# Two attention and expert layers on one core: loads, stores and output halves moved across phase ends, and fewer semaphore clears

## The reference

```python
x = x + tanh(g_xattn[l]) * attention_l(layernorm(x), ctx_1024, ctx_1024, Wq, bq, Wk, bk, Wv, bv, Wo, bo)
x = x + tanh(g_ffn[l])   * experts_l(layernorm(x), ...)
```

## Time and profile before

| what | before |
|---|---|
| median of 3 runs | 800.38 us (799.07 to 803.17) |
| profiled execution | 800.45 us |
| its span, first to last instruction | 798.7 us |
| busy: TensorE, its weight loads | 739.7 us (93%), 622.6 us (78%) |
| busy: VectorE, ScalarE, GpSimd | 586.2, 461.2, 372.5 us (73%, 58%, 47%) |
| mean granted TensorE clock | 0.969 of full |
| phases in the span, us | attention 1 to 211, route and experts 1 to 487, attention 2 489 to 683, route 2 to 698, experts 2 to 797 |

### The profile page before, as it was taken

One profiled execution on the slowest core, in us unless ns is written; L12 is line 12 of the kernel. 1 busy time (PEld: TensorE's weight loads), 2 busy tenths in 40 slices (PEclk: granted clock), 3 DMA queues, 4 the chain that ended last, 5 costly groups with the idle time before them and its releaser, 6 DMA issues. The chain is left out here.

```text
span 798.7 us, 17138 instructions
## 1 busy us (share of the span) xinstructions
PE 739.7 (93%) x6750; PEld 622.6 (78%) x6750; DVE 586.2 (73%) x1219; ACT 461.2 (58%) x701; POOL 372.5 (47%) x371
## 2 busy tenths in 40 slices
PE   6999999999899999999999983999999999779995
PEld 5666767666899999999999983656666567779994
DVE  5777777682469898898898862677777767759981
ACT  3476666756267776676676642467666754245640
POOL 5454555123044777676666534545545211033633
PEclk9999999999999999999999995999989999979998
DMA  7110000001059988888888625200000000579732
GB/s 221 31 45 26 29 29 27 29 29 55 27 194 366 271 262 269 267 271 268 254 279 272 183 47 156 72 29 28 16 2 16 15 29 15 175 248 318 202 80 27
DMA packets 47680, 103.44 MB, mean 129 GB/s; under 512 B 9936, under 2 KB 38224, under 8 KB 39920
## 3 DMA queue, kind: packets, MB, share of 16 engines
q0 software_dynamic: 16800, 65.46, 27.5%
q1 hardware_dynamic: 30800, 36.87, 13.9%
HBM read 84.22 MB, written 17.83 MB: 128 GB/s over the span
## 5 line engine op out<-in xcount | busy, mean ns | idle before, releaser
L928 DVE TENSOR_REDUCE mx_a<-ps_max_a 128x2 f32<-128x512 f32 x256 | 164.3, 685 | 43.8 <-PE ps_max_a L1238 42.8
L732 ACT ACTIVATE prob_a<-ps_st_a 128x2048 f32<-128x2048 f32 x64 | 120.1, 1877 | 40.4 <-PE ps_st_a L1257 40.1
L88 PE MATMUL ps_h_e<-xe_t_e,w_e 128*128 128x256 f32 x368 | 106.3, 289 | 6.3 <-DVE xe_t_e L2358 6.3
L90 PE MATMUL ps_h_e<-xe_t_e,w_e 128*128 128x256 f32 x368 | 103.4, 281 | 0.0
L89 PE MATMUL ps_h_e<-xe_t_e,w_e 128*128 128x256 f32 x368 | 103.4, 281 | 0.0
L1238 PE MATMUL ps_max_a<-k_r_a,q_r_a 32*128 32x512 f32 x256 | 86.4, 524 | 4.5 <-DVE mx_a L928 1.4
L90 PE MATMUL ps_y_e<-w_e,h_early 128*128 128x256 f32 x312 | 86.7, 278 | 0.0
L2134 POOL DMA_INDIRECT xe_e<-normalised_weighted,token_of x53 | 61.7, 1164 | 43.6 <-DMA normalised_weighted<-comb_first 18.3
L1257 PE MATMUL ps_st_a<-q_s_a,k_s_a 32*128 32x256 f32 x1024 | 79.8, 404 | 0.2
L2166 POOL DMA_INDIRECT x<-y_e,token_of x39 | 66.3, 1699 | 27.3 <-ACT y_e L2229 14.1
L553 POOL TENSOR_SCALAR r_var_eps_a<-r_mean_var_a 128x2 f32<-128x2 f32 x16 | 3.6, 228 | 158.5 <-DVE r_mean_var_a L955 158.5
(11 more groups left out here) (375 smaller groups left out, 2058.4 us busy)
## 6 DMA issues: line engine op xcount, KB each, us to landing
w_raw_w<-L_w SPq DMA_DIRECT2D x14, 1024.0 KB, 7.1
normalised_weighted<-xr SPq DMA_DIRECT2D x16, 256.0 KB, 2.2
x_sb<-x SPq DMA_DIRECT2D x8, 256.0 KB, 4.1
ctx_raw_a<-ctx_t SPq DMA_DIRECT2D x8, 256.0 KB, 4.5
x_sb<-x SPq DMA_DIRECT2D x2, 1024.0 KB, 8.2
x<-x_sb SPq DMA_DIRECT2D x8, 256.0 KB, 2.5
later_values<-x_sb SPq DMA_DIRECT2D x8, 256.0 KB
ctx_raw_a<-later_values SPq DMA_DIRECT2D x8, 256.0 KB, 3.4
```

What stands on the lines that cost most here:

```text
L88: pe.matmul(out, lhs[0], rhs[0], start=start, stop=False)
L90: return pe.matmul(out, lhs[0], rhs[1], start=False, stop=stop)
L732: act.activation(prob[n % 2][:, :, :, :], ps_st[:, :, :, :], ACT.Exp, scale=HD ** -0.5).then_inc(prob_ready, 1)
L928: dve.tensor_reduce(mx[:, q, h:h + HG + 1:HG], ps_max[j][:, :, :], AX.X, ALU.max).then_inc(max_done, 1)
```

## The change

Five things change.

1. Each `route_and_experts` makes one `semaphores` call instead of three, so one clear and barrier follow it. Semaphores that were allocated outside a phase are handed to the phase that clears them.
2. The first three x loads of the second attention are issued by SyncE at the end of the first expert stage, after the wait for the last landings.
3. The second layer's first three expert weight loads are issued in the second attention after the last batch's maxima (their buffers and semaphores now live from before attention), and the store of the first ten tiles' combination weights after the next row store.
4. The last two blocks, not the last alone, are handed over by halves, in both layers (`late`). The second halves go to a bank of the transposed inputs, `ps_x`, and wait for `xe_ready` of the last block instead of for the reading of another block's output.
5. The route's last fillers are 48 instead of 40.

```diff
+AHEAD = 3
...
-def semaphores(nc, ctx):
-    taken = []
+def semaphores(nc, ctx, handed=()):
+    taken = list(handed)
...
...
             "token_at": sb("token_at", [P, 2, LISTED, FIRST_TILES], F16),
+            "w1_raw": [sb(f"w1_raw{i}", [P, KC * F]) for i in range(2)], "w2_raw": sb("w2_raw0", [P, FC * D]),
+            "w1_ld": [nc.alloc_semaphore(f"w1_ld{i}_first") for i in range(2)], "w2_ld": nc.alloc_semaphore("w2_ld0_first"),
+            "comb_stored": nc.alloc_semaphore("comb_stored_first")}
...
-            load_x(0)
+            if layer == 0:
+                load_x(0)
...
-                load_x(1)
-                load_x(2)
                 sp.dma_start(bv[:, :], dram["bv"]).then_inc(wv_ld, 16)
...
+            def load_expert_weights():
+                sp.dma_start(early["w1_raw"][0][:, :], dram["w1"][0:P, :]).then_inc(early["w1_ld"][0], 16)
+                sp.dma_start(early["w2_raw"][:, :], dram["w2"][0:P, :]).then_inc(early["w2_ld"], 16)
+                sp.dma_start(early["w1_raw"][1][:, :], dram["w1"][P:2 * P, :]).then_inc(early["w1_ld"][1], 16)
+
+            def store_first_comb():
+                sp.wait_ge(first["comb_ready"], 1)
+                sp.dma_start(dram["xw"][0:FIRST_TILES * P, D:D + E].rearrange("(t p) e -> p t e", p=P),
+                             early["comb"][:, 0:FIRST_TILES, :]).then_inc(early["comb_stored"], 16)
...
             maxima_to_slots(B - 1)
+            if layer:
+                load_expert_weights()
             store_router_rows(B - 3)
+            if layer:
+                store_first_comb()
             store_router_rows(B - 2)
...
     def sync_part(sp):
-        for n, b in (("w1", 0), ("w2", 0), ("w1", 1)):
-            sp.dma_start(buffers[n + "_raw"][b][:, :], dram[n][b * P:b * P + P, :]).then_inc(buffers[n + "_ld"][b], 16)
         comb_dst = dram["xw"][0:N, D:D + E].rearrange("(t p) e -> p t e", p=P)
-        sp.dma_start(comb_dst[:, 0:FIRST_TILES, :], comb[:, 0:FIRST_TILES, :]).then_inc(tiles["comb_stored"], 16)
         sp.wait_ge(last["comb_ready"], 1)
...
-        fill_rows(40)
+        fill_rows(48)
...
+    def late(b):
+        return b >= blocks - 2
+
+    def late_halves(b):
+        return order[blocks - 2][2] if b == blocks - 1 else 0
+
+    def late_bank(b, q):
+        return ps_x[b % 2][:, 0, :] if q else ps_y[b % 2][:, 0, :]
...
+        if layer == 0:
+            x_src = dram["x1"][0:N, :].rearrange("(t p) d -> p t d", p=P)
+            for i in range(AHEAD):
+                tiles_of = slice(i * QT, i * QT + QT)
+                sp.dma_start(shared["x"][:, tiles_of, :], x_src[:, tiles_of, :]).then_inc(shared["later_x_ld"][i], 16)
...
-                if b == blocks - 1:
-                    pool.wait_ge(last_ready, q + 1)
+                if late(b):
+                    pool.wait_ge(last_ready, late_halves(b) + q + 1)
...
-                bank = ps_y[b % 2]
-                if b == blocks - 1 and q:
-                    wait(pe, y_ready if layer else y_biased, b)
-                    bank = ps_y[(b + 1) % 2]
+                out = late_bank(b, q) if late(b) else ps_y[b % 2][:, q, :]
+                if late(b) and q:
+                    pe.wait_ge(xe_ready, blocks)
...
-                if b == blocks - 1:
+                if late(b):
                     ins.then_inc(last_ps, 1)
...
-        buffers = expert_buffers(nc, ctx, layer)
-        tiles, experts = expert_phase(nc, ctx, layer, shared, dram, buffers, early)
+        new_sem = semaphores(nc, ctx, early["w1_ld"] + [early["w2_ld"], early["comb_stored"]] if layer else ())
+        buffers = expert_buffers(nc, ctx, layer, new_sem, early)
+        tiles, experts = expert_phase(nc, ctx, layer, shared, dram, buffers, early, new_sem)
...
+        shared["later_x_ld"] = [nc.alloc_semaphore(f"later_x_ld{i}") for i in range(AHEAD)]
```

More of the change, by code:

```diff
@@ L301, in ps @@
             return ctx.enter_context(nc.psum_tensor(f"{name}_a{layer}", shape, F32))
-        new_sem = semaphores(nc, ctx)
+        new_sem = semaphores(nc, ctx, shared["later_x_ld"] if layer else ())
         def sem(name):
@@ L352, in attention_phase @@
         ps_head, ps_lin = ps("ps_head", [P, 512]), ps("ps_lin", [P, 512])
-        x_ld = [sem(f"x_ld{i}") for i in range(XP)]
+        x_ld = shared["later_x_ld"] + [sem(f"x_ld{i}") for i in range(AHEAD, XP)] if layer else [sem(f"x_ld{i}") for i in range(XP)]
         wq_ld, wk_ld, wv_ld, wo_ld = (sem(n) for n in ("wq_ld", "wk_ld", "wv_ld", "wo_ld"))
@@ L1581, in _, with expert_buffers @@
             pool.wait_ge(ident_ready, 8)
-def expert_buffers(nc, ctx, layer):
-    sem = semaphores(nc, ctx)
+def expert_buffers(nc, ctx, layer, sem, early):
     def sb(name, shape, dt=F32):
@@ L1592, in pair @@
         return [sb(f"{name}{i}", shape) for i in range(2)]
-    buffers = {"w1_raw": pair("w1_raw", [P, KC * F + (0 if layer else FC)]),
-               "w2_raw": pair("w2_raw", [P, FC * D + (0 if layer else D)]),
-               "w1_ld": [sem(f"w1_ld{i}_w{layer}") for i in range(2)], "w2_ld": [sem(f"w2_ld{i}_w{layer}") for i in range(2)]}
+    if layer:
+        buffers = {"w1_raw": early["w1_raw"], "w2_raw": [early["w2_raw"], sb("w2_raw1", [P, FC * D])],
+                   "w1_ld": early["w1_ld"], "w2_ld": [early["w2_ld"], sem("w2_ld1_w1")]}
+    else:
+        buffers = {"w1_raw": pair("w1_raw", [P, KC * F + FC]), "w2_raw": pair("w2_raw", [P, FC * D + D]),
+                   "w1_ld": [sem(f"w1_ld{i}_w0") for i in range(2)], "w2_ld": [sem(f"w2_ld{i}_w0") for i in range(2)]}
     if layer:
@@ L1610, in gather_weights, with route_phase @@
                             ).then_inc(buffers[which + "_ld"][b % 2], 16)
-def route_phase(nc, ctx, shared, dram, buffers, tiles, early):
+def route_phase(new_sem, shared, dram, buffers, tiles, early):
     ident = shared["ident"]
@@ L1885, in route_phase, with later_route_phase @@
     return {"sync": sync_part, "gpsimd": pool_part, "scalar": act_part, "tensor": pe_part, "vector": dve_part}
-def later_route_phase(nc, ctx, shared, dram, buffers, tiles, early):
+def later_route_phase(new_sem, shared, dram, buffers, tiles, early):
     ident, comb = shared["ident"], early["comb"]
@@ L1990, in later_route_phase, with expert_phase @@
     return {"sync": sync_part, "gpsimd": pool_part, "scalar": act_part, "tensor": pe_part, "vector": dve_part}
-def expert_phase(nc, ctx, layer, shared, dram, buffers, early):
+def expert_phase(nc, ctx, layer, shared, dram, buffers, early, new_sem):
     ident = shared["ident"]
@@ L2155, in add_to_tokens @@
         def add_to_tokens(b):
-            if b < blocks - 1:
+            if not late(b):
                 pool.wait_ge(y_ready, b + 1)
```

28 lines of the change are left out of this document (13 added, 15 removed).

## The result

The changed kernel takes 790.85 us in the median of 4 executions (790.28 to 795.99), the kernel before, in the same series, 801.77 (799.07 to 806.73): 0.988 of its time, 95% interval 0.984 to 0.992. A later series of six more (the ninth experiment) gave 792.62, ratio 0.991 (0.988 to 0.995); over all ten the median is 791.5. The prediction was 787.3, range 783.0 to 792.5. The profiled execution took 790.28 us, with a span of 788.2 against 798.7. An execution takes longer than its span, and by more than before: 2.0 us in the mean of the changed kernel's ten, 1.7 in the 51 of the kernel before. So 0.3 us of what the span gains isn't in the time.

A forecast was written before the change was run, and what follows sets the result against it. TensorE is busy nearly all the span, so only its waits can pay. Second attention's start 6.0, route 2.3 and 1.6, tail 3.2 sum to 13.1 us off 800.38, giving 787.3 us, range 783.0 to 792.5.

The forecast's parts named there:

- the route's part: Second route: gathers start 2.3 us earlier, released by the token list, and 1.6 us less is lost to the low clock.
- End of stage 1: First expert stage's end: block 21 by halves brings the last scatter and its landing 2.3 us earlier.
- GpSimd starts 0.3 later: First expert stage's end: block 21's first scatter is issued 0.3 us after ScalarE weighs its first half, at about 474.0.
- Clears: End of each expert stage: one clear and barrier instead of three saves 1.0 us.
- x loads: Second attention's start: x lands before the phase opens; SyncE's issues give back about 0.8 us; queries begin 6.0 earlier overall.
- Rival 1: Second attention's start: fillers at the low clock hold it, gain there 3.7 us, time 789.7 us; chance 0.17.
- Route, the wait: Second route: the combination-weight store no longer queues behind weights, the token list becomes the bound, gathers start 2.3 us earlier.
- rival 3: Second route: the small store is slow by itself, not behind the weights; B gives nothing, 791.2 us; chance 0.06.
- Route, the clock: Second route's first products: the shorter TensorE gap wins half of 3.1 us lost at the low clock, 1.6 us.
- rival 2: Second route: the clock doesn't fall, so the route gains 5.4 us, time 785.8 us; chance 0.15.
- Tail: Kernel's end: block 5 by halves brings its last scatter 2.26 us earlier, fewer clears 1.0, together 3.2 us.
- rival 4: Second attention: the clock falls in more batches, 2.2 us each; seven more give 802.7 us; chance 0.02 in full.

The follow-up runs named there:

- ninth experiment: The changed kernel run again with nothing changed; 792.62 us in the median of six, ratio 0.991 to the kernel before.
- fourth run: The changed kernel with three semaphore calls in each expert stage, so three clears and barriers after it; 791.5 us, ratio 0.990.
- first: The changed kernel with the three weight loads and the first ten tiles' combination-weight store back in the second route; 796.5 us, ratio 0.994.
- seventh runs: The changed kernel with only the three weight loads back in the second route, the first ten tiles' store still in attention; 793.8 us, ratio 0.991.
- sixth: The changed kernel with the second expert's weight split moved behind the last pass-through tiles and the first inputs' split in the second route; 790.9 us, ratio 0.986.
- tenth: The changed kernel with all six pass-through tiles right after the token list, three weight splits, inputs' split, then the fourth; 44 fillers; 789.8 us.
- twelfth runs: The changed kernel with pass-through tiles after the token list, first expert's splits, inputs' split, second expert's splits last; 44 fillers; 787.9 us, ratio 0.985.
- eighth run: The changed kernel with 16 fillers instead of 24 at the second attention's start; 789.4 us, ratio 0.987.
- fifth run: The changed kernel with 64 fillers instead of 48 before the second route's first transposes and 12 before the first product; 788.4 us, ratio 0.987.
- The four undone parts: The changed kernel with one part undone each: route's DMAs, 796.5 us; x loads, 792.0; second-to-last block's halves, 794.6; single clear, 791.5.

## Why the prediction was right

Each part gained at the wait that the forecast named, and the time fell within the range, 3.6 us above the forecast value. In size the route's part fell short most: 2.1 us of 3.9, and so it came behind the tail, not before it. Profile against profile the span gained 10.5 us of 13.1, the time 10.2. This pair is a favourable one: over all executions the medians differ by 8.8 us, and the six of the ninth run alone have a median of 792.62, just above the range. By the steps of the forecast:

- **End of stage 1: 2.3 forecast, 2.0 measured** (last scatter against VectorE's last split, 9.97 before and 7.97 after). The step that was off is "GpSimd starts 0.3 later": block 21's first half has to wait for block 20's landing, which the split brought forward to be the last. The ninth run's row names the landing.
- **Clears: 1.0 at each end forecast, 0.7 to 1.0 measured** (fourth run, and 5.9 against 6.7 us at the end in the changed kernel). Of the second gain 0.3 is lost outside the span, which the forecast took as unchanged at 1.7 us; the fourth run gives back 0.2 of it, so most of that goes with the single clear. The changed kernel's one clear takes 1.2 us from the end barrier to the phase's start, the three of before 2.0.
- **x loads: the landings hid as forecast**, SyncE's 1.39 us of issues cost 0.7 of the 0.8 named, and the 12 fillers ran at the full clock. Start to queries was forecast within 0.1 us. Rival 1 didn't come in this profile; in the ninth run's it came in part, with 7.4 us from start to queries instead of 6.6.
- **Route, the wait: 2.3 forecast, 1.7 measured.** That the store was late because of the weights, and that the list would be the bound, is shown by the first and seventh runs; rival 3 falls. The gathers start even 2.8 earlier, since the first one follows the list by 0.29 us, where it followed the store's landing by 0.83. But their two issues take 1.3 longer, a cost that I didn't look for: the 4.6 us of VectorE's splits lay beside the wait for the store before, and the gathers came after most of them. Moved earlier, the gathers meet the splits. The sixth, tenth and twelfth runs show it by moving the splits.
- **Route, the clock: 1.6 forecast, about 0.4 measured** (the gain at the last output is 7.6, at the transposes 7.2). The clock fell in this profile, at 696.1, and rose at 703.0, 8.4 us earlier than before, while the first product started 7.6 us earlier: 5.4 us at the low clock instead of 6.2. The forecast took half of the stretch as won because the gap is shorter. The eighth run's profile has the same pauses and no low clock at the products, and the fifth run's has the low stretch ahead of them without a pause. So rival 2 does occur, in some executions, and is worth 2.5 us to the products when it does; the pauses alone don't decide it.
- **Tail: 3.2 forecast, 2.9 measured** (2.2 and 0.7).
- **The batches of attention** (rival 4): a new fall cost 2.6 us in the first two batches, and two old ones didn't come. That they cancel in this pair of profiles is luck. Over all executions the mean clock of the changed kernel is 0.973 and that of before 0.970, so 6.8 of the 8.1 us between the mean times remain at the common clock.

By the Trainium skill, page "TensorE: Matmul & The Clock Gate", section "HAM oscillation", it is long idle gaps of TensorE that bring the slow clock. The eighth run's route agrees, the changed kernel's own, with pauses of the same 1.7 and 1.5 us and a low stretch behind them, doesn't; here the measurement decides, and what makes the difference between the two stays open.

The four undone parts add up, at the common clock, to 1.7 + 0.2 + 2.8 + 0.9 = 5.6 us of these 6.8. What is left, 1.2, is about one standard error of the sum. It may also belong to the eight more fillers, which weren't tried alone, or to the x loads, of which the whole time showed nothing.

## What to carry to other kernels

When a wait is taken away, look at what ran beside it: the work that it hid now lies beside the step that was waiting, and can slow it. A head start gained ahead of a stretch at the low clock can be worth as little as half, if the clock rises at the same time in spite of it. Where the clock makes one kernel's times spread by 1%, read small gains as distances within a stage, and compare times with their mean clock beside them.

## What the runs showed of the hardware

GpSimd's issue of an indirect gather of 128 rows takes 0.95 us alone, 1.1 beside pass-through tiles of 0.42 us, and 1.8 to 3.5 beside VectorE's subtractions of 128x1024 (1.2 us each, up to three during one issue). It isn't a fixed rate. In the kernel before and in the first and seventh runs the first gather begins 0.1 to 0.25 us before the end of a split; it took 1.25, 1.11 and 1.17, though the next split ran beside the rest of it. In the changed kernel the first two begin with 0.85 and 0.99 of a split to go and take about 0.9 longer than alone. So most gathers are held for what is left of the split in which they begin. The third gathers of the tenth and twelfth runs, which begin 0.4 before a split's end, are held through the splits behind it as well, 2.5 and 1.4 us in all. What makes these differ stays open. The Trainium skill, page "SBUF — State Buffer", section "Who interferes with whom", has a VectorE instruction with two inputs in SBUF block a GpSimd instruction that reads SBUF until it is done; the gather reads its list there. The trace agrees in that short instructions beside it cost 0.15 us and three long ones 2.5, but not in the gathers that a following split left alone.

In a single kernel, unchanged, the low clock came at 508.4 to 518.7 in one execution and at 617.4 to 624.2 in another, with TensorE busy for 9.6 and 10.1 of the 10.4 us ahead of it; ten executions had mean clocks of 0.961 to 0.979 and times of 788.9 to 796.8 us.
